# Two graph layers on one core: VectorE's and ScalarE's small steps of the attention rounds set at other units, and the copies of turned tiles divided anew

## The reference, cut to what matters

```python
h  = relu(layernorm(x))                                # the kernel's h, from y
xp = einsum('mn,bnf->bmf', L_norm, h)
x1 = relu(layernorm(xp @ Wc + bc) * g1 + be1) + h      # z, z_std, z_gain, z_norm, x1
q, k, v = x1 @ Wq, x1 @ Wk, x1 @ Wv                    # 4 heads of 32
scores = where(adjacency > 0, q @ k.T / sqrt(32), -1e9)
attn = softmax(scores)
o  = (attn @ v) @ Wo + bo
x2 = layernorm(x1 + o) * g2 + be2                      # z2, z2_std, z2_gain, x2
out = x + layernorm(x2 + gelu(x2 @ W1 + b1) @ W2 + b2) * g3 + be3
```

## Time and profile before

| | before |
|---|---|
| time, median of 3 runs | 1019.43 us (1019.34 to 1019.48) |
| the profiled execution | 1022.98 us, span 1021.2 us |
| TensorE busy | 932.9 us, 91% of the span |
| VectorE busy | 630.3 us, 62% |
| ScalarE busy | 519.3 us, 51% |
| GpSimd busy | 325.5 us, 32% |
| mean granted TensorE clock | 0.955 of full speed |

### The profile page before, as it was taken

How to read it: one execution, slowest core, us unless ns; L and a number is a source line. 1 busy time by engine, 2 the same in 40 slices (tenths; PEclk the granted TensorE clock), 3 DMA queues, 4 the chain that set the end, 5 groups by cost and what they waited for, 6 DMA issues and landing times. The chain is left out here.

```text
span 1021.2 us, 19958 instructions
## 1 busy us (share of the span) xinstructions
PE 932.9 (91%) x7030; PEld 749.2 (73%) x7030; DVE 630.3 (62%) x2077; ACT 519.3 (51%) x1127; POOL 325.5 (32%) x405
## 2 busy tenths in 40 slices
PE   5998899999999999999699999999999999979982
PEld 4556799999999999988477777777777777656651
DVE  3752333333333333524588888988888888764998
ACT  2222322222222232210688888888888887765540
POOL 0001111111111111203234555544455543226775
PEclk8887999999999999989799999999999999998996
DMA  3000000000000000004354444444444444500111
GB/s 90 1 1 10 11 1 21 10 10 10 10 10 10 10 10 10 12 1 121 85 135 114 120 114 122 116 115 117 111 125 112 117 125 125 125 2 11 52 44 60
DMA packets 47218, 61.54 MB, mean 60 GB/s; under 512 B 4377, under 2 KB 22050, under 8 KB 47138
## 3 DMA queue, kind: packets, MB, share of 16 engines
q1 hardware_dynamic: 47138, 60.51, 22.9%
HBM read 39.53 MB, written 20.97 MB: 59 GB/s over the span
## 5 line engine op out<-in xcount | busy, mean ns | idle before, releaser
L1540 ACT ACTIVATE prob<-prob,low 128x512 f32<-128x512 f32 x256 | 184.0, 719 | 51.5 <-DVE low L1590 49.5
L1590 DVE CUSTOM_DVE_ANT_0 prob<-bank,mask 128x512 f32<-128x512 f32 x256 | 171.3, 683 | 28.3 <-PE bank L1419 26.7
L1432 PE MATMUL bank<-ident,prob 128*128 128x128 f32 x1024 | 161.9, 281 | 12.5 <-ACT probT L1529 12.3
L1432 PEld LDWEIGHTS bank<-ident,prob 128*128 128x128 f32 x1024 | 113.9, 141 | 58.3 <-issue 31.2
L1419 PE MATMUL bank<-k_stack,q_stack 128*128 128x512 f32 x256 | 123.8, 485 | 9.9 <-DVE low L1590 5.0
L1529 ACT ACTIVATE probT<-bank 128x512 f32<-128x512 f32 x176 | 102.5, 583 | 2.8 <-PE bank L1432 1.1
L1065 DVE TENSOR_TENSOR T_lo<-bank,T_hi 128x512 fp32r<-128x512 f32 x48 | 33.0, 688 | 112.0 <-ACT T_hi L903 112.0
L601 POOL TENSOR_SCALAR var_eps<-mv 128x4 f32<-128x4 f32 x16 | 3.6, 226 | 297.3 <-DVE mv L1018 297.3
L903 ACT ACTIVATE T_hi<-bank 128x512 fp32r<-128x512 f32 x48 | 28.4, 592 | 134.7 <-PE bank L813 91.7
L909 ACT ACTIVATE Sq<-bank,trace_inv 128x512 fp32r<-128x512 f32 x64 | 43.9, 686 | 92.3 <-PE bank L736 92.3
L1452 PE MATMUL bank<-probT,v 128*32 128x128 f32 x2048 | 82.3, 279 | 3.1 <-ACT probT L1529 1.1
(11 more groups left out here) (232 smaller groups left out, 1943.9 us busy)
## 6 DMA issues: line engine op xcount, KB each, us to landing
k_stack<-bounce_q SPq DMA_DIRECT2D x64, 256.0 KB, 5.0
q_stack<-bounce_k SPq DMA_DIRECT2D x64, 256.0 KB, 7.5
bounce_q<-k_parts SPq DMA_DIRECT2D x16, 512.0 KB, 2.8
bounce_k<-q_parts SPq DMA_DIRECT2D x16, 512.0 KB, 3.2
x_in<-in_x_dram SPq DMA_DIRECT2D x16, 256.0 KB, 2.7
out_dram<-result SPq DMA_DIRECT2D x16, 256.0 KB, 2.2
A<-in_adj_dram SPq DMA_DIRECT2D x4, 256.0 KB, 3.2
W1s<-in_L_gnn_W_dram SPq DMA_DIRECT2D x1, 128.0 KB, 2.2
```

The source lines that it names most:

```text
L1432: last = pe.transpose(psum[2 + u % 2][:, mt * P:(mt + 1) * P], prob[u % RING][:, mt * P:(mt + 1) * P], ident[:, :])
L1540: act.activation(prob[u % RING][:, :], prob[u % RING][:, :], ACT.Exp, bias=low[:, u % TURNED:u % TURNED + 1], scale=-1.0, accum_out=row_su ...
L1590: dve.tensor_tensor_reduce(prob[u % RING][:, :], psum[u % 2][:, :], mask[:, u // HEADS, :], 1.0, 3e38, ALU.add, ALU.min, low[:, u % TURNED ...
```

## The change

Only constants and one position in GpSimd's list change. VectorE's `y_moments` moves from u = 9 to u = 0 (there it stands after the copy of unit 13 and ahead of the reciprocal); the moments of z2 move from u = 3 to u = 4 (after the low part of k), and z2_std from u = 5 to u = 8 (after the product with the spread inverses, `AT_O`). The four pieces of h on ScalarE move from units 11, 12, 13, 15 to 10, 11, 12, 13. VectorE copies the turned tiles 3, 6, 10, 12, 13 (at u = 6, 9, 13, 15, 0) where it copied 0, 7, 11, 13, 15 (at u = 3, 10, 14, 0, 2); ScalarE copies the rest, still eleven. On GpSimd `h_scales` moves from behind the normalisation of the finishing batch to ahead of it. The waits follow the lists by `copied` and are otherwise the same.

```diff
-AT_Y_MOMENTS, AT_H = 9, (11, 12, 13, 15)
+AT_Y_MOMENTS, AT_H = 0, (10, 11, 12, 13)
 AT_RINV, AT_SPREAD, AT_SPREAD_OUT, AT_O, AT_PROJ, AT_Z2 = 0, 3, 4, 8, 11, 12
-AT_Z2_MOMENTS, AT_Z2_STD = 3, 5
+AT_Z2_MOMENTS, AT_Z2_STD = 4, 8
 TURN_LAG = 3
 VALUES_LAG = 7
 VALUES_STEP = 2
-DVE_COPIES = (0, 7, 11, 13, 15)
+DVE_COPIES = (3, 6, 10, 12, 13)
...
                     if within(r, 1, BATCH - 2):
                         split_h(r + 1, 1 - s)
+                    if within(r, 0, BATCH - 3):
+                        h_scales(pool, one, r + 2, s)
                     e = r - 3
                     if within(r, 3, BATCH + 2):
                         inverse_root(pool, e, mv_c, c_mv, ve_c, rstd_c, c_pool, z2_std_ready, e, exponent, pool_waited)
...
-                    if within(r, 0, BATCH - 3):
-                        h_scales(pool, one, r + 2, s)
                     if enters:
                         add_bo(r, s)
```

## The result

The changed kernel takes 1036.17 us (median of four, 1034.75 to 1040.72) against 1019.45 us: 1.0177 times the time before, with an interval of 1.0140 to 1.0215. That is 16.7 us slower; the forecast was 22.8 us slower, 1042 us with a range of 1031 to 1052.

The account below looks back on a forecast made before the run. A round was taken as a loop of mostly VectorE's work from z2 to u = 3, then TensorE's; 1.3 + 1.5 + 20.9 + 1.7 + 0.5 - 3.1 = +22.8 us on 1019.43 gave 1042 us, range 1031 to 1052.

Parts of the forecast that it names:

- VectorE's stretch: VectorE from z2 to mask 2: y_moments and a copy come in, small waits go; 8.66 us becomes 10.37.
- The residual: VectorE's residual in steady rounds: kept at 1.06 us because it still meets GpSimd's cast; free of it, 0.38 less a round.
- ScalarE's 0.47: ScalarE at u = 2: tile 15's copy stands between the exponential and x1T_out, adding 0.47 us a round.
- TensorE's wait at u = 7: Value products' weight loads at u = 7: the wait goes because VectorE copies tile 3; 0.3 us a round (nothing to 0.57).
- Round 1: First attention round: no z2 before it, so it pays y_moments alone, 1.3 us.
- Round 17's -3.1: End of the attention block: with z2_std behind the product with the spread inverses, z2 comes earlier; -3.1 us (-2.4 to -6).
- Rounds 14 and 15: Rounds without y_moments: 0.5 us, plus about 1.2 for q's low part behind z2's moments; 1.7 together.
- round 16: Late round: copies shift to ScalarE's full units 2 and 3, costing 0.5 us (0 to 1.5).
- The clock: Rival inside the rounds: TensorE's close waits at u = 2 and 3 halve its clock; 1046 to 1062 us, 12 in 100.
- Faster: Rival in the rounds: VectorE's stretch doesn't pace, added work vanishes and waits go; 1005 us, 8 in 100.
- q's stacks: q_stack's transfers before a round's first scores: room shrinks from 1.7 us to about 1.1, costing nothing.
- milder: Rival in the rounds: residual escapes GpSimd, tile 15 is hidden, u = 7 wait worth 0.57; +12 us, 1031, 12 in 100.

Follow-up runs that it names:

- y_alone: The kernel before with only y_moments moved from u = 9 to u = 0: 1035.09 us, 1.0141 times before, a round of 27.34 us.
- x1_first: The kernel before with GpSimd waiting for x1 at the head of a round, before spreading inverses and splitting h: 1013.55 us, 0.9953 times before.
- z2_std_only: The kernel before with only z2_std moved from u = 5 to u = 8: 1018.08 us in one execution, a round of 26.05 us.
- copies_alone: The kernel before with only the turned tiles' copies divided as in the changed kernel: 1020.18 us, 1.0022 times before.
- tile15_back: The kernel before with VectorE copying tiles 3, 6, 10, 13, 15, so 15 stays VectorE's and 12 ScalarE's: 1017.20 us in one execution.
- after_again: The changed kernel, unaltered, run once more for its scatter: 1033.30 us (1031.75 and 1034.84).
- z2_alone: The kernel before with only z2's moments moved to u = 4 and z2_std to u = 8: 1014.49 us, 0.9936 times before.
- all_but_y: The kernel before with the new copies, z2's moments at u = 4 and z2_std at u = 8: 1019.88 us, 1.0005 times before.
- z2_x1_first: The kernel before with z2's moments at u = 4, z2_std at u = 8 and GpSimd waiting for x1 each round: 1007.64 us, 0.9897 times before.

## Why the prediction was right, and where its sizes were off

**The loop was read rightly.** The bound is VectorE's list from z2 to mask 2, then ScalarE's to x1T_out, then TensorE's. y_alone lengthens only the first way, tile 15 the second, z2_std only the last, and each change of a part shows up whole in the round.

**VectorE's stretch: forecast 10.37, measured 10.05.** Over eleven rounds this is 3.5 us, the largest term of the 6.1 by which the forecast was too high. The residual was kept at 1.06 us because GpSimd's work follows it along; that work does follow, but it meets another piece of it: start to start the residual takes 0.76 instead of 0.98, which is 0.22 of the 0.32. The bound given for it was 0.38, and 0.38 is what a residual that meets nothing gains (x1_first). The Trainium skill (GPSIMD Engine Reference, Specifications) names the contention, and the runs agree: 0.69 us with GpSimd waiting, 1.07 with its copy and cast beside it. In the kernel before GpSimd's copy starts 0.09 us ahead of the residual, since both had to wait for GpSimd's z_norm:

```profile
678.27 0.61 POOL L1373 COPY rinv<-sums_inv 128x512 f32<-128x512 f32 x1
```

In the changed kernel z_norm is early, and the copy starts as soon as the reciprocal is done, 0.31 us ahead of the residual (690.40):

```profile
690.09 0.61 POOL L1373 COPY rinv<-sums_inv 128x512 f32<-128x512 f32 x1 [1.36 <-DVE sums_inv L1606]
690.64 1.07 POOL L1363 CAST h_hi<-h 128x512 fp32r<-128x512 f32 x1
```

In each kernel without the wait of x1_first the residual ends 0.60 us after the start of the cast, whether it takes 1.07, 0.88 or 0.84; the cast takes 1.07 us there and 0.62 in x1_first. That reads as if copy, residual and cast went one behind the other in the order of their starts; no run was made to test it. The other 0.10 of the stretch are differences of 0.01 to 0.03 us in its other steps.

**ScalarE's 0.47: measured 0.48.** Tile 15 in front of x1T_out costs the same with and without the rest of the change.

**TensorE's wait at u = 7: 0.3, measured 0.32, for the wrong reason.** The prediction gave it to tile 3's new owner. z2_std at u = 8 alone removes it (z2_std_only), tile 3 on VectorE alone removes most of it (copies_alone, tile15_back), and both together don't remove more. So z2_std, costed at nothing, was a gain of the change, and the copies without it are a loss of 0.35. That the size fits is luck: it was the middle of a guess, put to the wrong step.

**The edges.** Round 1 cost more than was forecast. From the block's first instruction, ScalarE's L_hi (489.86 before, 489.06 after), to mask 0 of round 2 it is 28.07 and 29.39 us, +1.32 for +1.3; but this agreement is luck. In that profile of the changed kernel VectorE's L_lo took 2.29 us, where it took 3.40 before; in after_again it took 3.40 too, and the same way is 30.33 us, +2.26, of which y_alone (29.54) shows 1.47. The rest of it wasn't followed up. Of the -1.92 in the table 0.80 lies ahead of L_hi and 1.12 is that L_lo. Round 17's -3.1 is -3.15, but the forecast gave it all to z2_std: that step alone gives 2.15 (z2_alone), the copies alone 1.82, and both together 3.16 (all_but_y), so here too the size is partly luck. Rounds 14 and 15 were set too dear by 0.9, and round 16 has the wrong sign: +0.5 was forecast for ScalarE's full units 2 and 3 and -1.46 came, as in copies_alone and tile15_back (-1.6). There no batch enters, so no x1T stands behind tile 15; that tiles 12 and 15 have no part in it tile15_back shows, and that it is the tiles freed at u = 6 and 9 is read off, not tested alone.

**The rivals.** The clock fell once inside eleven rounds (0.51 from 579.20 on, behind a wait of 1.24 us for a mask) and not at all in after_again, although TensorE waits 0.9, 0.25 and 0.9 us close together. That round took 28.72 us instead of 27.92; in after_again the same round has the same wait of 1.24 and takes 28.23 at the full clock, so the fall cost about 0.5. The Trainium skill's warning of a clock that halves in each pass (TensorE: Matmul & The Clock Gate, HAM oscillation) is not borne out here: ten of eleven rounds show the full 2.4 GHz. "Faster" failed on what was held against it: z2 can't start before its projection, and the stretch had 0.2 to 0.3 us of slack for 1.94 that came in. q's stacks landed 0.8 us or more before the first scores of every round from 2 to 14, so the transfers didn't become the bound. The "milder" rival, +12 us, was nearer to the measured 16.7 than the main case: of its three terms the residual gave 0.22 of 0.38, tile 15 nothing of 0.47, and the wait at u = 7 0.32 of 0.57.

## What to carry to other kernels

When every engine waits a little, find the loop that closes a round and measure its ways one by one; a step is dear or free by the way on which it lies, and not by the load of its engine: the same 1.34 us of VectorE's work cost 0.97 a round more at u = 0 than at u = 9 (y_alone), and 0.18 more at u = 3 (in z2_x1_first). Follow a wait back past the engine that ended it: the copy that TensorE waited for at u = 7 was late for an exponential that was late for a mask that stood behind a step nobody needed yet. And look for work of GpSimd beside VectorE's instructions on the critical list: letting GpSimd wait for one of them won 0.34 us a round.

## What the runs showed that was not expected

Which of two colliding instructions pays can turn over from one execution to the next of the same kernel. At the start of the block VectorE's L_lo (two SBUF inputs, 2048 columns) runs beside GpSimd's h_lo. VectorE's and GpSimd's timelines of the changed kernel in its first profile:

```profile
491.00 2.29 DVE L1639 TENSOR_TENSOR L_lo<-adjT,L_hi 128x2048 fp32r<-128x2048 f32 x1 [6.04 <-ACT L_hi L1565]
```

```profile
491.00 3.42 POOL L1365 TENSOR_TENSOR h_lo<-h,h_hi 128x512 fp32r<-128x512 f32 x1
```

and in after_again:

```profile
484.65 3.40 DVE L1639 TENSOR_TENSOR L_lo<-adjT,L_hi 128x2048 fp32r<-128x2048 f32 x1 [6.04 <-ACT L_hi L1565]
```

```profile
484.65 1.26 POOL L1365 TENSOR_TENSOR h_lo<-h,h_hi 128x512 fp32r<-128x512 f32 x1
```

Once VectorE takes 2.29 us and GpSimd 3.42, once VectorE 3.40 and GpSimd 1.26, as in the kernel before. The traces keep the starts to the nanosecond, and so show which came first. In the two profiles in which VectorE's L_lo took 2.29 beside h_lo (this one and tile15_back) it had started 0.004 us earlier; in the seven in which it took 3.39 or 3.40, GpSimd's h_lo had started 0.007 to 0.020 us earlier. In the four kernels with the wait of x1_first the two don't meet, and L_lo takes 2.29. So the one that starts first keeps its own time, and the other is longer by about the first one's (1.1 and 2.2 us), which is also how the residual, the copy and the cast behave above. That the order of starts decides is read from nine traces; no run shifted one against the other.
